# Two more broadcasts as DMA inside SBUF, and a new order of the feed-forward tasks

## What is computed

```python
x = x + 0.5 * ffn(layernorm(x))      # wqkv, q_scale, k_scale, wo, ln_g, ln_b, w1, b1, w2, b2
x = x + attn(layernorm(x))           # latent attention, 16 heads, causal
x = x + 0.5 * ffn(layernorm(x))      # the same weights again

def ffn(x):                          # two layers
    h = shift_token(x)               # the upper 64 channels come from the token before
    q, k, v = split(h @ wqkv)        # 8 heads of 64
    q, k = rotary(l2norm(q) * qs, l2norm(k) * ks)
    o = local_attention(q, k, v)     # windows of 64: own and previous, softmax
    x = x + o @ wo
    h = shift_token(x)
    h = (h - mean) / sqrt(var + 1e-5) * lg + lb
    a, g = split(h @ w1 + b1)
    return x + (a * gelu(g)) @ w2 + b2
```

## Time and profile before

| | |
|---|---|
| median of three runs | 2167.96 us |
| the profiled execution, its own time | 2170.55 us |
| its span, first to last instruction | 2168.7 us |
| mean granted TensorE clock | 0.955 |
| PE, DVE, ACT, POOL busy | 82%, 69%, 51%, 42% of the span |
| DMA queue of the kernel | 115.79 MB, 31.8% of 16 engines |

### The profile page before, as it was taken

One profiled execution on the slowest core, in us unless ns is written; L12 is line 12 of the kernel. 1 busy time (PEld: TensorE's weight loads), 2 busy tenths in 40 slices (PEclk: granted clock), 3 DMA queues, 4 the chain that ended last, 5 costly groups with the idle time before them and its releaser, 6 DMA issues. The chain is left out here.

```text
span 2168.7 us, 50695 instructions
## 1 busy us (share of the span) xinstructions
PE 1785.8 (82%) x20074; PEld 1079.9 (50%) x20074; DVE 1488.3 (69%) x2281; ACT 1112.0 (51%) x2070; POOL 905.7 (42%) x624
## 2 busy tenths in 40 slices
PE   1578888888888886899999997578888888888885
PEld 1344444555555543566666664344454455555543
DVE  2567777677666753688888886567777677766752
ACT  1134444454544542688888886234444454544542
POOL 2445544555445540332233321445544555445530
PEclk9889999999999998899999998689999999999998
DMA  4234434544455441000000000334344544355441
GB/s 140 37 58 71 69 62 76 77 80 69 71 79 81 73 68 36 1 1 2 1 2 1 2 1 1 37 63 72 63 71 70 81 75 74 66 85 84 84 72 40
DMA packets 66076, 119.03 MB, mean 55 GB/s; under 512 B 13183, under 2 KB 23603, under 8 KB 63667
## 3 DMA queue, kind: packets, MB, share of 16 engines
q1 hardware_dynamic: 65843, 115.79, 31.8%
HBM read 49.55 MB, written 3.28 MB: 24 GB/s over the span
## 5 line engine op out<-in xcount | busy, mean ns | idle before, releaser
L786 DVE SCALAR_TENSOR_TENSOR TP<-bank,cols,tab 128x1024 f32<-128x1024 f32 x256 | 318.4, 1274 | 51.5 <-PE bank L450 42.5
L946 POOL TENSOR_TENSOR QK<-QK,RB 128x1024 f32<-128x1024 f32 x128 | 302.4, 2363 | 118.6 <-DMA RB<-RN 118.6
L940 POOL TENSOR_TENSOR QK<-TP 128x512 f32<-128x512 f32 x128 | 164.9, 1289 | 327.4 <-DVE TP L786 291.3
L1205 ACT ACTIVATE PL<-bank,NM 128x384 f32<-128x384 f32 (+3 forms) x512 | 255.7, 539 | 15.8 <-DVE NM L1286 13.0
L1286 DVE TENSOR_REDUCE NM<-bank 128x1 f32<-128x384 f32 (+3 forms) x352 | 217.9, 635 | 35.6 <-PE bank L1119 31.7
L809 DVE TRANSPOSE_TENSOR_REDUCE MX<-bank 128x16 f32<-128x512 f32 x256 | 160.2, 681 | 118.3 <-PE bank L487 118.3
L642 ACT ACTIVATE SQ<-bank 128x512 f32<-128x512 f32 x128 | 76.5, 598 | 275.7 <-PE bank L450 275.5
L1128 PE MATMUL bank<-cst,PL 128*128 128x128 f32 x1280 | 199.7, 275 | 3.6 <-DVE PTL L1295 1.4
L827 DVE TENSOR_TENSOR OT<-bank,OT 128x512 f32<-128x512 f32 x128 | 85.3, 687 | 160.9 <-DMA OT<-sums_d 146.9
L1114 PE MATMUL bank<-KL,QZL 128*128 128x384 f32 (+3 forms) x512 | 189.8, 422 | 2.3 <-DVE QZL L1242 2.3
L648 ACT ACTIVATE SQ<-bank 128x512 f32<-128x512 f32 x128 | 76.5, 598 | 201.2 <-DVE TP L786 201.2
(11 more groups left out here) (169 smaller groups left out, 3655.8 us busy)
## 6 DMA issues: line engine op xcount, KB each, us to landing
RB<-RN SPq DMA_DIRECT2D x512, 64.0 KB, 4.0
OT<-sums_d SPq DMA_DIRECT2D x128, 256.0 KB, 4.0
V<-V SPq DMA_DIRECT2D x32, 512.0 KB, 6.0
V<-V SPq DMA_DIRECT2D x32, 384.0 KB, 7.1
RB<-vars_d SPq DMA_DIRECT2D x32, 256.0 KB, 3.2
X<-in_L_attn_x SPq DMA_DIRECT2D x8, 256.0 KB, 4.6
out<-X SPq DMA_DIRECT2D x8, 256.0 KB, 4.7
wqkv_raw<-in_L_ffn_wqkv SPq DMA_DIRECT2D x1, 1536.0 KB
```

Source lines behind the costliest of these rows:

```text
L786: nc.vector.scalar_tensor_tensor(out=TP[:, o:o + 2, :], in0=BK[4 + z][:, :].unsqueeze(1).to_broadcast([P, 2, T]), scalar=q, in1=tab[:, e, ...
L940: nc.gpsimd.tensor_tensor(QK[:, m, 0, :], TP[:, 2, :], TP[:, 1, :], ALU.subtract)
L946: nc.gpsimd.tensor_tensor(QK[:, m, :, :], QK[:, m, :, :], RB[:, m, :].unsqueeze(1).to_broadcast([P, 2, T]), ALU.mult).then_inc(S["nr_ok"], 1)
L1205: last = nc.scalar.activation(PL[:, m % PRING, h * N:(h + 1) * N], BK[m % SRING][:, h * N:(h + 1) * N], ACT.Exp, bias=NM[:, m % SRING, h:h ...
```

## The change

The sums no longer pass through DRAM. SP issues four DMAs per g, each copying one partition of DR (0, 32, 64 or 96) to 64 partitions of OT, 128 KB. DR gets two halves, one per g. The variances no longer pass through DRAM either: four DMAs, each copying one partition of RV to the 128 partitions of a quarter of HNL, 64 KB. HNL takes RB2's place, so SP waits until PE has read the HNL of the unit before. `sums_d`, `vars_d` and RB2 are gone. Each j has a semaphore of its own, d_in0 to d_in3. No arithmetic changes.

```diff
@@ -116,8 +116,6 @@
-sums_d = nc.dram_tensor("sums_d", (2, LG, T), F32).ap()
-vars_d = nc.dram_tensor("vars_d", (2, NT, P), F32).ap()
@@ -329,14 +327,13 @@
-DR = sb("DR", [P, T])
+DR = sb("DR", [P, 2, T])
-RB2 = sb("RB2", [P, T])
@@ -378,25 +375,25 @@
     sp.dma_start(V1[W:P, 1:NT, :], V0[W:P, 0:NT - 1, :]).then_inc(S["v1_ok"], 16)
 
 def sums(u, g):
-    n = 2 * u + g
-    sp.wait_ge(S["dl_ok"], n + 1)
-    sp.dma_start(sums_d[n % 2], DR[0:P:32, :]).then_inc(S["d_out"], 16)
-    sp.wait_ge(S["d_out"], 16 * (n + 1))
+    sp.wait_ge(S["dl_ok"], 2 * u + g + 1)
     if u >= 1:
         sp.wait_ge(S["wo_in"], u)
-    for e in range(2):
-        src = sums_d[n % 2].rearrange("(j e) n -> e j n", e=2)[e]
-        sp.dma_start(OT[W * e:W * e + W, 2 * g:2 * g + 2, :],
-                     src.unsqueeze(0).broadcast_to([W, 2, T])).then_inc(S[("d0_in", "d1_in")[g]], 16)
+    for j in range(2):
+        for e in range(2):
+            h = 2 * j + e
+            sp.dma_start(OT[W * e:W * e + W, 2 * g + j, :],
+                         DR[32 * h:32 * h + 1, g, :].unsqueeze(1).broadcast_to([1, W, T])
+                         ).then_inc(S[f"d_in{2 * g + j}"], 16)
 
 def variances(u):
     sp.wait_ge(S["vn_ok"], u + 1)
-    sp.dma_start(vars_d[u % 2], RV[0:P:32, :]).then_inc(S["rv_out"], 16)
-    sp.wait_ge(S["rv_out"], 16 * (u + 1))
-    if u >= 1:
-        sp.wait_ge(S["hn_ok"], u)
-    src = vars_d[u % 2].rearrange("(a k) n -> a (k n)", a=1)
-    sp.dma_start(RB2[:, :], src.broadcast_to([P, T])).then_inc(S["rb_in"], 16)
+    if u >= 1:
+        sp.wait_ge(S["w1a_in"], 3 * u)
+        sp.wait_ge(S["w1g_in"], 3 * u)
+    for t in range(NT):
+        sp.dma_start(HNL[:, t * P:(t + 1) * P],
+                     RV[32 * t:32 * t + 1, :].unsqueeze(1).broadcast_to([1, P, P])
+                     ).then_inc(S["rb_in"], 16)
 
 def result(u):
     b = u - NB
@@ -672,11 +669,12 @@
 def sums(u, g, k):
     n = 2 * u + g
     act.wait_ge(S["dd_in"], n + 1)
-    if n >= 1:
-        act.wait_ge(S["d_out"], 16 * n)
-    nc.scalar.activation(DR[:, :], BK[k][:, :], ACT.Ln).then_inc(S["dn_ok"], 1)
+    if u >= 1:
+        act.wait_ge(S[f"d_in{2 * g}"], 32 * u)
+        act.wait_ge(S[f"d_in{2 * g + 1}"], 32 * u)
+    nc.scalar.activation(DR[:, g, :], BK[k][:, :], ACT.Ln).then_inc(S["dn_ok"], 1)
     act.wait_ge(S["dn_ok"], n + 1)
-    nc.scalar.activation(DR[:, :], DR[:, :], ACT.Exp, scale=-1.0).then_inc(S["dl_ok"], 1)
+    nc.scalar.activation(DR[:, g, :], DR[:, g, :], ACT.Exp, scale=-1.0).then_inc(S["dl_ok"], 1)
 
 def square_c(u, k):
     act.wait_ge(S["dt_in"], u + 1)
@@ -689,7 +687,7 @@
 def variance(u):
     act.wait_ge(S["vv_ok"], u + 1)
     if u >= 1:
-        act.wait_ge(S["rv_out"], 16 * u)
+        act.wait_ge(S["rb_in"], 64 * u)
     link(nc.scalar.activation(RV[:, :], VV[:, :], ACT.Ln))
     nc.scalar.activation(RV[:, :], RV[:, :], ACT.Exp, scale=-0.5).then_inc(S["vl_ok"], 1)
 
@@ -823,7 +821,7 @@
 
 def attended(u, j, k):
     dve.wait_ge(S["pv_in"], 4 * u + j + 1)
-    dve.wait_ge(S[("d0_in", "d1_in")[j // 2]], 32 * (u + 1))
+    dve.wait_ge(S[f"d_in{j}"], 32 * (u + 1))
     nc.vector.tensor_tensor(OT[:, j, :], BK[k][:, :], OT[:, j, :], ALU.mult).then_inc(S["ot_ok"], 1)
 
 def residual(u, k):
@@ -949,8 +947,8 @@
 
 def hidden(u):
     pool.wait_ge(S["s2_ok"], u + 1)
-    pool.wait_ge(S["rb_in"], 16 * (u + 1))
-    nc.gpsimd.tensor_tensor(DC[:, :], DC[:, :], RB2[:, :], ALU.mult).then_inc(S["hn_ok"], 1)
+    pool.wait_ge(S["rb_in"], 64 * (u + 1))
+    nc.gpsimd.tensor_tensor(DC[:, :], DC[:, :], HNL[:, :], ALU.mult).then_inc(S["hn_ok"], 1)
 
 def low_hidden(u):
     pool.wait_ge(S["hnh_ok"], u + 1)
```

More of the change, by code:

```diff
@@ L412, in _ @@
                         for n in range(-3, NU + 4):
[L413 to L416, removed]
+                            run(values, n - 1)
                             run(result, n - 4)
-                            run(values, n - 1)
+                            run(variances, n - 2)
+                            run(sums, n - 1, 0)
+                            run(sums, n - 1, 1)
+                            run(norms, n)
                         if store:
@@ L582, in _ @@
                         for n in range(-3, NU + 4):
[L583 to L601, removed]
                             run(attend, n - 2, 3, 5)
-                            run(values, n - 1, 0, 6)
                             run(values, n - 1, 1, 7)
-                            run(values, n - 1, 2, 6)
+                            run(values, n - 1, 2, 4)
                             run(values, n - 1, 3, 7)
+                            run(hidden, n - 3, 1, 0, 4)
                             run(hidden, n - 3, 1, 1, 6)
-                            run(hidden, n - 3, 0, 0, 4)
+                            run(back, n - 4, 5)
+                            run(tokens, n + 1, 5)
                             run(join, n - 2, 7)
@@ L611, in _ @@
                             run(scores, n - 1, 0)
[L612 to L615, removed]
+                            run(center, n - 2, 7)
+                            run(project, n, 1)
+                            run(hidden, n - 3, 1, 2, 6)
+                            run(variance, n - 2, 7)
+                            run(turn_max, n - 1, 0, 6)
+                            run(hidden, n - 3, 0, 0, 7)
+                            run(add_max, n - 1, 0)
+                            run(hidden, n - 3, 0, 1, 6)
+                            run(project, n, 2)
+                            run(hidden, n - 3, 0, 2, 7)
+                            run(scores, n - 1, 1)
+                            run(sums, n - 1, 0, 7)
+                            run(project, n, 3)
+                            run(turn_max, n - 1, 1, 6)
+                            run(outward, n - 3, 7)
+                            run(add_max, n - 1, 1)
+                            run(norms, n, 6)
+                            run(attend, n - 1, 0, 7)
+                            run(sums, n - 1, 1, 5)
+                            run(attend, n - 1, 1, 7)
+                            run(attend, n - 1, 2, 6)
+                            run(values, n, 0, 4)
                     @block.scalar
@@ L737, in _ @@
[L737 to L741, removed]
+                            run(values, n - 1, 2, 4)
+                            run(values, n - 1, 3, 7)
+                            run(high, n)
+                            run(gate, n - 3, 0, 4)
+                            run(square_a, n, 0)
@@ L743, in _ @@
+                            run(sums, n - 1, 0, 7)
+                            run(high_hidden, n - 2)
+                            run(square_a, n, 3)
+                            run(square_b, n, 3)
+                            run(softmax_exp, n - 1, 1)
+                            run(norms, n)
+                            run(sums, n - 1, 1, 5)
+                            run(values, n, 0, 4)
+                            run(values, n, 1, 7)
                     @block.vector
@@ L888, in _ @@
                         for n in range(-3, NU + 4):
-                            run(gated, n - 4, 2, 6)
+                            run(rotate, n - 1, 0, 0)
+                            run(maxima, n - 2, 0)
+                            run(rotate, n - 1, 1, 1)
+                            run(add_eps, n - 3, 7)
+                            run(spread_max, n - 2, 0, 6)
+                            run(rotate, n - 1, 1, 0)
+                            run(gated, n - 4, 0, 7)
+                            run(gated, n - 4, 1, 6)
@@ L898, in _ @@
-                            run(tokens, n)
                             run(clamp, n - 1, 6)
-                            run(attended, n - 2, 0, 5)
+                            run(statistics, n + 1)
+                            run(attended, n - 2, 0, 7)
                             run(norms, n - 1)
[L902 to L905, removed]
+                            run(attended, n - 2, 1, 7)
@@ L906, in _ @@
+                            run(tokens, n + 1)
+                            run(attended, n - 2, 2, 6)
                             run(attended, n - 2, 3, 5)
-                            run(gated, n - 3, 0, 4)
+                            run(back, n - 4, 5)
+                            run(arrive, n + 1, 5)
                             run(residual, n - 2, 7)
                             run(rotate, n, 0, 1)
-                            run(rotate, n, 0, 0)
-                            run(maxima, n - 1, 0)
@@ L912, in _ @@
[L912 to L917, removed]
                     @block.gpsimd
@@ L964, in _ @@
                         for n in range(-3, NU + 4):
+                            run(norms, n - 3, 2)
+                            run(rotate, n - 2, 0)
                             run(norms, n - 3, 3)
```

44 lines of the change are left out of this document (17 added, 27 removed).

## The result

The changed kernel takes 2692 us, the median of four runs (2676.64 to 2697.11), against 2169: 1.240 times as long, with a 95% interval of 1.236 to 1.244. The profiled execution took 2676.64 us, the shortest of the four; its span is 2674.8 us, its mean granted clock 0.861.

What follows compares the result with a forecast made beforehand. Waits on the DMA queue between sums and norms were taken to bound the kernel; 30 periods 11.5 us longer (345) plus 25 for drains, added to 2170.55, gave 2540.6, forecast 2540 us, range 2190 to 2790.

Steps and rivals of the forecast that it cites:

- rival 2: Sums and variances: no overlap inside a pair of transfers, 16.1 and 8.1 us per group; 2790 us, chance 0.20.
- What bounds the kernel: Feed-forward loop: waits, not a full engine; a third of the 44.3 us period, sums to norms, is the DMA queue.
- Price of one source: Broadcast from a single SBUF partition: 27 GB/s, so 64 KB alone takes 2.4 us plus 1.6 latency.
- Price of a group of sums: Four 128 KB transfers of sums from single partitions: 12.9 us, between 6.2 and 19.4; through DRAM 1.8.
- The new period: One feed-forward unit, summed from maxima to PE's scores: 57.9 us against 46.4, 345 us over 30 periods.
- SP's wait for HNL and ACT's new waits: SP's variances wait for the previous unit's hidden, ACT's waits are for transfers a unit old: both cost nothing.
- ACT's queue behind `high_hidden`: high_hidden, waiting for variances and POOL, stands before the third squares: squares end at 23.8, clamp at 26.4 us.
- Fill and drain: Ends of both feed-forward phases: a lone variances and two sums each, 13 us more per phase, 25 in all.
- Order: Statistics and tokens leave the stretch from maxima to clamp: units below 8 gain 3.8 us, reaching the others' 44.3.
- The signs: In the new profile: OT landings far over 4 us, waits of several hundred us, DMA share near 0.9, L661 58 apart.
- Rival 1: Sums and variances overlap as well as RB's rotating sources, 6.2 and 3.1 us per group; 2191 us, chance 0.25.
- Rival 3: 27 GB/s was only a start-up matter, so transfers are fast and the round trip is saved; 2105 us, chance 0.08.

Runs made afterwards that it cites:

- e6: Changed kernel with sums, variances and norms each copied from many source rows, and transfers of sums and norms joined into fewer, larger ones: 1993 us, 0.918.
- the probe: Kernel before, with groups of broadcasts from chosen rows timed alone at the end of setup: 6.3 us for one transfer, 4.6 to 20.7 for four of 128 KB.
- e10: Changed kernel with ACT's high_hidden moved behind the squares of m = 3: 2619 us, 1.206, 73 us below the changed kernel.
- e2: Changed kernel with its new order of tasks, but sums and variances through DRAM as before: 2120 us, 0.977.
- e12: e6 with ACT's high_hidden moved behind the squares of m = 3: 1992 us, 0.920.
- e11: Changed kernel with sums through DRAM as before and ACT's high_hidden behind the squares of m = 3: 2193 us, 1.011; without that move 2305 us.

## Why the prediction was right or wrong

The forecast of 2540 was 152 us too low. 2692 lies within the range of 2190 to 2790, but outside the 2400 to 2680 that the prediction gave to its own case, and nearer to rival 2 (2790). Of the 136 us by which the profiled execution exceeds the 2540.6 summed for it, 85 lie in the 30 periods and 51 in fills and drains. The direction and the path were right, the price of the sums and that of the drains were too small.

- **What bounds the kernel: right.** The stretch from the sums to the norms closed the period, and it is the stretch that grew. e6, which shortens it, wins 8%.
- **Price of one source: right, from one window.** 27 GB/s became 25 to 27 in the probe (the four neighbours; 4.7 us of the 6.3 for one transfer of 131 KB, less 1.6 of latency, is 28).
- **Price of a group of sums: too small. This is the term that failed.** The step "two thirds of 4.85 us each" put 12.9 us; the term of both groups was 25.8 and measured 28.8, 14.4 each. It took the overlap of RB's transfers, whose four source rows are 8 apart, for that of rows 0 and 32, which overlap hardly: 14.0 us against 18.9 in the probe by swapping two of them.
- **The new period: 57.9 summed, 61.8 in the period shown.** Against maxima(0) = 475.13: RV is ready at 10.2 (11.8 predicted); variances landed at 20.6 (20.8); clamp ends at 27.8 (26.4); last sums landed 49.4 (45.8); the multiply for m = 1 ends at 58.7 (54.8); next maxima at 61.8. The squares held by `high_hidden` came as forecast (23.5 for 23.8), but PE's norms took 3.42 us for 1.92 before: PE had idled 3.87 us for the squares, and in 499 to 501 us its granted clock was 0.50, the lower of its two levels (1.2 GHz), for 1.00 before. The 3.6 us of the sums carry nearly all of the difference at the end. `low`, costed at 0.7 at most and summed as nothing, was on the path: the eighth RB transfer landed at 530.7, the multiply began behind `low` at 531.4. The mean over both phases is 60.8.
- **SP's wait for HNL and ACT's new waits, costed at nothing: right, but narrowly for HNL.** SP issues the variances at 485.32, as soon as RV is ready. PE's `hidden` of the unit before had ended 0.4 us earlier, at 484.9.
- **ACT's queue behind `high_hidden`: seen, and its price was underrated.** It stood in the sum, but what it does to the filling of the queue did not: 73 us (e10).
- **Fill and drain: 25 predicted, 76 measured.** I had 13 us per phase for one variance and the sums behind the last mark. The prediction's own prices give more: 5.5 for the variances and 2 x 11.1 for two groups of sums, 27.7 a phase if nothing hides them, and behind the last mark of the second phase 31 were measured. Behind it stand the second sums of the unit before, the RB group, two sets of variances and two groups of sums, each slowed. Which of these carries how much was not taken apart.
- **Order: 3.8 us for units below 8, nothing for the others, 66 us in a world of free transfers; e2 measured 48.** The direction and the size are right: e2's marks are 43.2 to 45.1 us apart, but for the first two of each phase.
- **The signs.** OT<-DR at 11.0 us to landing, waits of several hundred us, the stretched issues (2.5 us in the median for OT<-DR) and marks alike for all units (60.1 to 65.5, but for the first of each phase) came as named. The DMA share did not near 0.9 over a whole period; it was 0.73 (470 to 531 us, 54 GB/s). Rival 2's sign, pairs that land 10 us apart, came weaker: the second group's pairs landed 7.8 us apart (OT at 516.73 and 524.53 above), where rival 2's price of a pair is 8.05 and the forecast's 6.4.
- **The rivals.** Rival 1 (RB's rotating rate) is out. Rival 2, no overlap inside a pair, has the mechanism right: rows 0, 32, 64, 96 take 18.9 us in the probe, 0, 64, 32, 96 take 14.0 and 0, 40, 80, 120 take 12.7. The port rule of the Trainium skill, "SBUF — State Buffer", section Door 1, has p and p+32 on one port. The probe agrees: rows 0 to 3, one port by that page, take 20.7, about four times the 4.7 of one. Rival 2's sum of 16.1 us per group was too low for a group alone (18.9, some 1.6 of it latency) and too high in the full queue (14.4), and its period of 65.9 is 5 too long. Building the forecast on it would have been nearer, but no hit: 2790 is 98 us too high, and its 35 us for the drains are 41 too few. That the stated range held is in part luck: 2692 had left the forecast's own case and lies in the half of rival 2 that the range took in. Rival 3 is out.

## What to carry to other kernels

A broadcast DMA whose source is one SBUF partition moved at 25 to 28 GB/s here, alone, with the DMA engines busy for 0.8 to 0.9 of the time. If a matmul with a block of ones or a reduction leaves equal rows, copy each to a few partitions instead; where only single rows will do, do not issue two that are 32 apart one after the other (18.9 us against 14.0). Price a transfer by its source partitions and by what is queued behind it, not by its bytes and its own latency alone; what its destination partitions are worth was not varied here. A task that waits for a transfer, ahead of other work on its engine, cost nothing with fast transfers (e6 and e12) and 73 to 112 us with slow ones (e10, e11), so order and transport must be tried together.

## What I had not expected of the hardware

Neighbouring partitions as sources do not help at all: rows 0 to 3 took 20.7 us, more than 18.9 for 0, 32, 64 and 96. The order of issue alone, 0, 64, 32, 96 for 0, 32, 64, 96, took 4.9 us off. A transfer of 128 KB from 32 rows inside SBUF lands in 2.6 us, and one of 256 KB from 64 rows in 3.6 (e6, OT<-DR), for 4.0 of the same 256 KB from DRAM before.

PE's granted clock fell while PE waited for the sums. It was 1.00 (2.4 GHz) up to 514 us; PE was busy for 0.49 of the 2 us before that and not at all in the 2 us behind it. From 516 to 528 us it was 0.50 (1.2 GHz). PE's join began at 525.27, on the lower clock, and by 530 us the granted clock was 1.00 again. From the lists of lines of before and after (busy us, mean ns):

```profile
L530 PE MATMUL bank<-OT,wo_s 128*128 128x512 f32 x256 | 117.9, 604 | 4.1 <-DVE OT L827 4.1
```

```profile
L527 PE MATMUL bank<-OT,wo_s 128*128 128x512 f32 x256 | 174.2, 843 | 57.5 <-DVE OT L825 57.5
```

So the slow transfers also lengthened matmuls, 56 us of them here. In the period shown this is hidden: the join ended at 530.84, and the scores that close the period waited for POOL's multiply until 533.8.
